# Expert outputs stored over the gathered rows, sixteen row buffers, and the late row scatters in one block

## The reference, cut to what matters

```python
probs = softmax(xt @ gate_w + gate_b)
_, idx = top_k(probs, 2)                       # 2 of 8 experts for each token
mask = (one_hot(idx).sum(axis=1) > 0)
h1 = relu(einsum('th,ehf->etf', xt, w1) + b1[:, None, :])      # 128 -> 512
out_e = einsum('etf,efh->eth', h1, w2) + b2[:, None, :]        # 512 -> 128
out = einsum('eth,te->th', out_e, mask)
```

## Time and profile before

| what | value |
|---|---|
| times of three executions | 623.2, 623.84, 632.16 us |
| median | 623.84 us |
| the profiled execution's own time | 632.16 us (the only one that is not below its span) |
| its span, first to last instruction | 630.1 us |
| busy, share of the span | PE 80%, DVE 65%, ACT 46%, POOL 43% |
| experts, first layer | about 203 to 293.5 us of the span |
| experts, second layer | about 528 to 617.3 us |

### The profile page before, as it was taken

One profiled execution on the slowest core, in us unless ns is written; L12 is line 12 of the kernel. 1 busy time (PEld: TensorE's weight loads), 2 busy tenths in 40 slices (PEclk: granted clock), 3 DMA queues, 4 the chain that ended last, 5 costly groups with the idle time before them and its releaser, 6 DMA issues.

```text
span 630.1 us, 14208 instructions
## 1 busy us (share of the span) xinstructions
PE 502.2 (80%) x4416; PEld 402.7 (64%) x4416; DVE 411.6 (65%) x1351; ACT 290.4 (46%) x824; POOL 269.1 (43%) x358
## 2 busy tenths in 40 slices
PE   4889998999973999893248899889789775998890
PEld 3656665656542999893136677667566465998890
DVE  5778888868867454536968646957956776643333
ACT  2234455435541665664354456625625312656650
POOL 3325543356475445646001133322822654355550
PEclk9979999858985899997576879979878755999995
DMA  7997000000001212213997000000000002212216
GB/s 231 336 286 322 3 2 1 1 10 27 5 32 48 79 52 78 76 52 116 373 292 293 2 2 1 2 1 2 28 9 3 27 28 64 67 57 78 78 39 208
DMA packets 28376, 53.71 MB, mean 85 GB/s; under 512 B 4817, under 2 KB 24209, under 8 KB 27249
## 3 DMA queue, kind: packets, MB, share of 16 engines
q1 hardware_dynamic: 23216, 42.17, 20.9%
q0 software_dynamic: 4544, 9.45, 4.2%
q10 hardware_dynamic: 544, 1.20, 0.6%
HBM read 42.32 MB, written 29.81 MB: 114 GB/s over the span
## 4 chain that ended last, share of the span: by engine, by line
PE 34%; DVE 30%; issue 16%; POOL 12%; DMA 4%; ACT 2%; SPq 1%; DVEq 1%; POOLq 0%; ACTq 0%
POOL ybuf L745 10%; DVE negm L870 5%; PE ps L2099 3%; PE ps L1999 3%; DVE X L1372 2%; PE ps L2059 2%; DMA w<-ybuf 2%; PE ps L2083 2%; PE ps L1845 1%; PE ps L1855 1%; POOL xbuf L695 1%; DVE rsc L944 1%; PE ps L1881 1%; PE ps L1915 1%; PE ps L2007 1%
## 5 line engine op out<-in xcount | busy, mean ns | idle before, releaser
L1579 ACT ACTIVATE probs<-ps,w1s 128x128 f32<-128x128 f32 x312 | 89.4, 376 | 58.4 <-PE ps L1999 47.7
L745 POOL DMA_INDIRECT ybuf<-yt,xg x78 | 77.5, 994 | 69.3 <-DVE yt L1126 58.2
L1999 PE MATMUL ps<-xgT,w1s 128*128 128x128 f32 x624 | 88.3, 287 | 8.9 <-DVE w1s L1062 7.3
L1999 PEld LDWEIGHTS ps<-xgT,w1s 128*128 128x128 f32 x624 | 80.2, 201 | 11.9 <-ACT xgT L1570 10.0
L2007 PE MATMUL ps<-w,probs 128*128 x624 | 82.2, 276 | 0.0
L780 POOL TENSOR_SCALAR_AFFINE_SELECT probs<-probs 128x512 f32<-128x512 f32 x64 | 39.4, 640 | 95.7 <-ACT probs L1680 95.6
L695 POOL DMA_INDIRECT xbuf<-rsc,sloti x64 | 62.5, 976 | 40.3 <-DVE sloti L999 15.2
L2007 PEld LDWEIGHTS ps<-w,probs 128*128 128x128 f32 x624 | 75.6, 192 | 0.0
L870 DVE TENSOR_REDUCE negm<-ps 128x2 f32<-128x512 f32 (+1 forms) x96 | 60.3, 685 | 22.3 <-PE ps L1832 17.1
L1493 ACT ACTIVATE probs<-ps 128x512 f32<-128x512 f32 x96 | 51.2, 600 | 35.5 <-PE ps L1855 35.1
L640 POOL TENSOR_SCALAR_AFFINE_SELECT probs<-probs 128x512 f32<-128x512 f32 x64 | 39.2, 637 | 60.6 <-ACT probs L1493 59.7
(11 more groups left out here) (280 smaller groups left out, 1115.1 us busy)
## 6 DMA issues: line engine op xcount, KB each, us to landing
xbuf<-in_c_pads SPq DMA_DIRECT2D x16, 1122.0 KB, 18.1
xg<-xbuf SPq DMA_DIRECT2D x78, 66.0 KB
w<-in_w SPq DMA_DIRECT2D x2, 2064.0 KB, 34.1
w<-in_w SPq DMA_DIRECT2D x2, 2048.0 KB, 35.7
w<-ybuf SPq DMA_DIRECT2D x8, 512.0 KB, 5.5
ybuf<-yt,xg POOLq DMA_INDIRECT x78
probs<-in_c_sel ACTq DMA_DIRECT2D x2, 512.0 KB, 5.2
bias<-in_b SPq DMA_DIRECT2D x2, 512.0 KB, 30.6
```

The lines of the kernel that those rows point to most:

```text
L745: pool.indirect_dma_start(out=ybuf[l][:, :], out_offset=bass.IndirectOffsetOnAxis(ap=xg[n % AHEAD][:, D:D + 1].bitcast(I32), axis=0), in_= ...
L1579: ins = act.activation(hidT[n % 3][:, c * P:(c + 1) * P], ps[:, q, c * P:(c + 1) * P], ACT.Gelu if l == 0 else ACT.Relu, bias=w[:, FF + c: ...
L1999: mm = pe.matmul(ps[:, n % 2, c * P:(c + 1) * P], w[:, c * P:(c + 1) * P], xgT[n % 2][:], start=True, stop=True)
```

## The change

The `yt` buffers are gone: the bias addition writes the result of tile n over the gathered rows in `xg[n % AHEAD]`, columns 0 to 127, and the scatter takes data and row numbers from the same buffer. `AHEAD` goes from 12 to 16. DVE no longer waits for a scatter; POOL does in its place, before it sends tile n, for that of tile n - 8, because eight scatter semaphores are left. At step 4 POOL sends the four late row scatters in one block, ahead of its wait for tile 4, and then y scatters alone, each as soon as its copy is done and POOL is free. Three semaphores are dropped: the pads of both layers share one, the table `pairs` is counted with the weights (thresholds 6 become 7), and an unused one goes.

```diff
-AHEAD = 12
+AHEAD = 16
...
-CAUGHT_UP = (12, 16, 20, 24)
...
-        yt = [sb(f"yt{r}", [P, D]) for r in range(DEPTH)]
...
-                sp.dma_start(xbuf[l][E * REGION:, :], inp["c_pads"][E * REGION:, :]).then_inc(pads_out[l], 16)
+                sp.dma_start(xbuf[l][E * REGION:, :], inp["c_pads"][E * REGION:, :]).then_inc(pads_out, 16)
...
-                pool.wait_ge(w_loaded[0], 16 * 6)
+                pool.wait_ge(w_loaded[0], 16 * 7)
...
                 def scatter_y(n):
+                    pool.wait_ge(m["y_copied"], n + 2)
                     pool.wait_ge(gathered[n % AHEAD], loads(l, n))
+                    if scatters(l, n % DEPTH, n // DEPTH) > 0:
+                        pool.wait_ge(scattered[n % DEPTH], scatters(l, n % DEPTH, n // DEPTH))
                     pool.indirect_dma_start(out=ybuf[l][:, :], out_offset=bass.IndirectOffsetOnAxis(ap=xg[n % AHEAD][:, D:D + 1].bitcast(I32), axis=0),
-                                            in_=yt[n % DEPTH][:], in_offset=None).then_inc(scattered[n % DEPTH], 16)
-
-                behind = 0
+                                            in_=xg[n % AHEAD][:, 0:D], in_offset=None).then_inc(scattered[n % DEPTH], 16)
+
                 for n in range(ET):
-                    pool.wait_ge(m["y_copied"], n + 2)
-                    if 0 <= n - LATE_ROWS < TOPK * size(LATE):
-                        t, k = divmod(n - LATE_ROWS, TOPK)
-                        ready_row(l, TILES[LATE][0] + t, LATE)
-                        scatter_row(l, TILES[LATE][0] + t, k)
-                        behind += 1
-                    else:
-                        scatter_y(n - behind)
-                    if n in CAUGHT_UP:
-                        behind -= 1
-                        scatter_y(n - behind)
+                    if n == LATE_ROWS:
+                        for t in range(*TILES[LATE]):
+                            scatter_rows(l, t, LATE)
+                    scatter_y(n)
...
                 def copy_y(n):
                     e = of_tile.pop(n)
                     dve.wait_ge(m["y_ready"], n + 2)
-                    if scatters(l, n % DEPTH, n // DEPTH) > 0:
-                        dve.wait_ge(scattered[n % DEPTH], scatters(l, n % DEPTH, n // DEPTH))
-                    dve.tensor_tensor(yt[n % DEPTH][:], ps[:, 6 + n % 2, 0:D], bias[:, ds(e * D, D)], ALU.add).then_inc(m["y_copied"], 1)
+                    dve.tensor_tensor(xg[n % AHEAD][:, 0:D], ps[:, 6 + n % 2, 0:D], bias[:, ds(e * D, D)], ALU.add).then_inc(m["y_copied"], 1)
```

More of the change, by code:

```diff
@@ L310, in build @@
         rows_out = [sem(f"rows_out{q}") for q in range(4)]
-        pads_out = [sem(f"pads_out_{l}") for l in range(2)]
-        pairs_loaded = sem("pairs_loaded")
+        pads_out = sem("pads_out")
         gathered = [sem(f"gathered{r}") for r in range(AHEAD)]
@@ L338, in build @@
         stats_done = sem("stats_done")
-        rstd_step = sem("rstd_step")
         stored = sem("stored")
@@ L556, in fill @@
                     rows_e = slice(e * REGION, (e + 1) * REGION)
-                    sp.dma_start(xbuf[l][rows_e, :], inp["c_pads"][rows_e, :]).then_inc(pads_out[l], 16)
-                sp.dma_start(xbuf[l][E * REGION:, :], inp["c_pads"][E * REGION:, :]).then_inc(pads_out[l], 16)
-            sp.dma_start(pairs[:].rearrange("p t k -> p (t k)"), inp["c_pairs"][:, :]).then_inc(pairs_loaded, 16)
+                    sp.dma_start(xbuf[l][rows_e, :], inp["c_pads"][rows_e, :]).then_inc(pads_out, 16)
+                sp.dma_start(xbuf[l][E * REGION:, :], inp["c_pads"][E * REGION:, :]).then_inc(pads_out, 16)
+            sp.dma_start(pairs[:].rearrange("p t k -> p (t k)"), inp["c_pairs"][:, :]).then_inc(w_loaded[0], 16)
             fill(0)
@@ L717, in _ @@
                 if (c, s) == (2, 2):
-                    pool.wait_ge(pairs_loaded, 16)
                     rank_constants()
@@ L723, in _ @@
                     if t == 0:
-                        pool.wait_ge(pads_out[0], 16 * (E + 1))
+                        pool.wait_ge(pads_out, 16 * (E + 1))
                     scatter_rows(0, t, q)
@@ L792, in _ @@
                         if t == 0:
-                            pool.wait_ge(pads_out[1], 16 * (E + 1))
+                            pool.wait_ge(pads_out, 2 * 16 * (E + 1))
                         scatter_rows(1, t, q)
@@ L1772, in gate_rows @@
                 if q == 0:
-                    pe.wait_ge(w_loaded[l], 16 * (6 if l == 0 else 4))
+                    pe.wait_ge(w_loaded[l], 16 * (7 if l == 0 else 4))
                 pe.wait_ge(m["rT_copied"], sum(rT_banks(a) for a in range(q + 1)) + 1)
```

## The result

The changed kernel takes 627.57 us (median of 20 runs, 622.67 to 634.57) against 624.25 us for the kernel before in the same measurement (20 runs, 617.29 to 632.16). The ratio is 1.0056, 95% interval [1.003, 1.0082]: a little slower, by less than 1%, 3.3 us between the medians, where 3.3 us faster was forecast. 627.57 lies above the range of 616 to 626. Medians in this document are of all executions, while a ratio leaves out those that lie more than 1.5% above the fastest of their kernel, so the two can disagree.

What follows compares the result with a forecast made beforehand. PE was taken to bound the expert stages at 1.90 us a tile. Gaps gained 7.3, less 3.8 for the long bunch and 0.2 for waits, gave 3.3 us: 623.84 - 3.3 = 620.5 us, range 616 to 626.

Steps and rivals of the forecast that it cites:

- Which engine bounds the stage: Expert stages: PE is always busy, one tile each 1.90 us; POOL keeps up and waits for DVE's copies.
- sizes of the bunch: POOL, once a layer: four late rows and y scatters, ten in a row at 1.26 us, 12.6 us.
- The term of 7.3 us for the eight gaps: PE's four gaps a layer at the catch-up steps vanish with the bunches of three scatters: 7.3 us gained at most.
- rival (1): Expert stages: gaps not from bunches in ordinary executions, nothing on the path changes, 623 to 624.5 us; 0.27 with (4).
- (4): Expert stages: the block goes before y4, nothing else moves; same time as rival (1), 0.27 together.
- The term of 3.8 us for the long bunch: Ten-scatter bunch beside PE: priced as two small gaps of 0.9 us, 1.9 us a layer, 3.8 us lost.
- rival (2): Long bunch holds PE's signals to its end: 5.0 us idle a layer, +2.9 us, 626.7; chance 0.13.
- Gaps of the triples did not add up within one: Argument against rival (2), from the gaps beside bunches of three scatters at the catch-up steps; no size.
- Most of it falls in the stretch that DVE's routing paces: Long bunch: mostly where DVE's routing sets 2.03 rather than 1.90 us a tile, so no more than 1.9 a layer.
- The terms at nothing: Gather lead, earlier late rows, merged semaphores and storing over gathered rows: 0 us each.
- The rule on the shared port: POOL's long bunch: each of six weight copies by DVE could add about half a microsecond, making no tile later.
- rival (3): Long bunch costs nothing and small gaps go too: 7.3 + 1.5 - 0.2 = 8.6 us gained, 615.2 to 617; chance 0.15.

Runs made afterwards that it cites:

- block only: Kernel before with POOL's new order alone (late row scatters in one block, then each y scatter as soon as copied), chip 7: 632.18 us, ratio 1.0069.
- old places: Changed kernel with four row buffers and a spacer placed so every other buffer lies where it lay before, chip 7: 638.35 us, ratio 1.0173.
- single rows: Changed kernel with late row scatters sent one by one at steps 4, 6, 8 and 9: 626.31 us on chip 15, 635.67 on chip 13.

## Why the prediction was wrong

**Which engine bounds the stage, and the sizes of the bunch: right.** POOL waits for DVE's copies as before (31.8 us in 31 waits against 29.5 in 24), the late rows and y scatters go at 1.26 us, and POOL has caught up about where 226.7 + 1.26 j = 222.0 + 2.03 j puts it: in the first profile after, four rows and seven y scatters run in a row from 234.41 before POOL waits 0.43 us, against ten scatters foreseen. No trace has a wait of DVE for a scatter, no turn of a tile in the later part of a stage waits for its gather, and the waits for gathers at the start add up to 0.7 us for 0.5.

**The term of 7.3 us for the eight gaps: the step that failed.** "3.6 + 3.7 = 7.3 us at most, if all of these gaps come from them" was taken at full size, and "I carry the difference over" made it the gain of every run. The gaps are real (on chips 7 and 13, too, a layer of POOL's old order has four, or two or three and one without a releaser), and where the triples go they go. But on chips 15, 9 and 5 no trace of either kernel has one, with the kernel before shown there on chip 9. There nothing can be won, and the kernel before shown with 83.5 and 82.3 us had no gap to lose. The one profile at hand came from a chip of the kind with gaps, or from an execution like it; the sign was in the text, the 8.3 us that the profiled execution stood above the median, and I gave the case built on it, rival (1), 0.27 together with (4). By the pair of chips 13 and 9 the kernel before differs by 633.97 - 624.59 = 9.4 us, and its expert stages by (87.8 + 87.1) - (83.5 + 82.3) = 9.1: most of the difference lies in these two stages (the stages are of single executions, which differ by 635.04 - 624.29 = 10.75 us), 6.2 us of it in gaps by a staged copy.

**The term of 3.8 us for the long bunch: too small where it counts.** Taken as two small gaps, 1.9 us a layer. On the chips that hold signals it measured 3.5 and 4.0 us (block only), 3.4 and 4.5 (old places), 4.3 and 4.6 (changed, chip 13). Rival (2) had this right, and nearly in detail: a bunch of six scatters, 6 x 1.26 = 7.6 us, for which 549.03 to 556.35 measured 7.3, and 5.0 us of idle PE, for which 4.3 and 4.6 stand. "Gaps of the triples did not add up within one" was no argument against it. "Most of it falls in the stretch that DVE's routing paces" failed too: in the second layer on chip 13 DVE stood idle for 4.90 us while PE's signals stood out, so its routing did not hide the gap.

What rival (2) lacked was the clock: the group behind the gap takes 2.05 us for 1.06. PE's busy time by stage shows what that costs. On chip 13, both layers, first the kernel before, then the changed one (columns as above):

```profile
209.00:297.00 88.00, 81.22 (x702) 78.71 (x702) 42.36 (x136) 56.36 (x201) 46.67 (x48) 0.96 0.22 65
531.00:618.00 87.00, 80.53 (x702) 78.39 (x702) 36.02 (x124) 51.63 (x196) 45.09 (x48) 0.97 0.23 65
...
212.00:300.00 88.00, 80.23 (x702) 77.89 (x702) 42.77 (x138) 56.58 (x201) 46.25 (x49) 0.97 0.24 66
531.00:621.00 90.00, 82.39 (x702) 81.06 (x702) 36.41 (x126) 51.94 (x196) 44.58 (x48) 0.93 0.23 63
```

In the second layer the gaps by a staged copy grew by 1.9 us, one of 0.93 us went, and the same 702 matmuls took 82.39 - 80.53 = 1.9 us more at the lower clock: 2.9, and the stage grew by 89.7 - 87.1 = 2.6. In the first layer the long gap came in two parts, 2.87 and 1.42 us, the clock stayed at 1.00 from 232 to 252, and PE's work was 1.0 us shorter, since the stage began at a granted clock of 0.88 (212 to 232) where the kernel before had 0.83 (209 to 229). The gaps grew by 0.8 and the stage shrank by 0.3. So in this pair of executions the long bunch cost 0.8 and 1.0 us more of idle PE than the small gaps had, and the larger loss is the clock of the second layer.

**The sum, as it came out.** On chips that hold signals: the small gaps gone, the large ones in their place, and on chip 13 the changed kernel is 3.6 us slower by medians against the 29 runs beside it and 4.5 against the 12 of the kernel before profiled with it; rival (2) worked out +2.9. On chips that hold none the medians lie 0.8 (chip 15), 0.5 (chip 9; 1.6 against the kernel before profiled there) and 0.9 (chip 5) apart, rival (1)'s zero to within what the runs can tell, with the same sign each time. The first measurement, +3.3, lies between the two kinds. The sign of the forecast would have needed a long bunch that costs less than the gaps it removes, on a chip that has gaps at all; no chip showed that.

**The terms at nothing: right, as far as they can be read.** Semaphores alone leave gaps and stages as they were (87.5 and 87.1 us); storing over the gathered rows alone too (87.7 and 86.5); old places do not bring the gaps back or drive them out. The extra wait on POOL, put at 0.1 us a layer, cannot be seen in any of these times.

**The rule on the shared port: there, but small.** The forecast let weight copies stretch the bunch by up to half a microsecond each. In the changed kernel's first profile, first layer, three scatters of the bunch took 1.17, 1.10 and 1.05 us and all others 0.95 to 0.98, 0.44 us more in all. What parts them is which of the two started first (timelines of DVE and POOL):

```profile
236.99 0.43 DVE L1052 COPY w1s<-w 128x516 f32 x1 [0.47 <-issue]
237.14 1.10 POOL L691 DMA_INDIRECT xbuf<-rsc,sloti  x1 [0.30 <-issue]
...
238.54 0.95 POOL L691 DMA_INDIRECT xbuf<-rsc,sloti  x1 [0.30 <-issue]
238.94 0.43 DVE L1052 COPY w1s<-w 128x516 f32 x1 [0.47 <-issue]
```

The scatter of 237.14 began inside a copy that ended at 237.42 and took 0.14 us more than 0.96. The scatter of 238.54 was under way when its copy began, and lost nothing. The other two long ones, at 234.41 and 247.40, began inside copies as well, and so did the one of 253.97 inside the addition of the earlier trace rows; all four end 0.82 to 0.83 us after the DVE operation does. The Trainium skill, SBUF - State Buffer, section "SBUF: two separate sides", lets GpSimd's descriptors wait until DVE's copy has ended. The trace agrees for a scatter that begins inside a copy; the price is what is left of the copy, 0.22 to 0.34 us here less some 0.13, and not half a microsecond for each copy beside the bunch.

**The chances and one term.** They do not add up as written: the halves of (2) and (3) that were left out come to 0.14 and not to two tenths, and for the 1.5 us in the sum of rival (3) the row behind it gives 1.1. Neither changes which case came out.

**What stays open.** Why some chips hold PE's signals beside a run of indirect scatters and others do not: it goes with the chip in every measurement here (held on 7, 3 and 13, free on 15, 9 and 5), but each chip was seen once. That the scatters hold them is argued from the order: on chip 7 POOL's order alone turned four small gaps in a layer into one long one at the new bunch. A kernel without bunches was never run on a chip of the first kind; both tries fell on chips 15 and 5. That single rows make the longest gap shorter (2.1 us and, in the second layer, 1.7, against 2.9 and 4.6 on chip 13; 635.67 us against 638.51) agrees with it. Which chips the first twenty runs of each kernel came from is not known, nor whether the 0.5 to 0.9 us on the free chips are anything (on chip 9 the interval of the ratio leaves 1 out, on chips 15 and 5 it does not). No version that I tried beats the kernel before: single rows are at 626.31 against 625.95 on chip 15 and at 635.67 against 634.92 on chip 13.

## What to carry to other kernels

A gap in one profile is a gain only if ordinary executions have it: where the profiled execution stands above the median by about as much as the gaps that you mean to remove, profile the same kernel again, on another chip too, before you build on them. Two profiles from different chips must not be subtracted stage by stage; a stage that the change can't touch (here the first attention, +13.3 us) is the control, and when it moves, the pair is no comparison. And where back-to-back indirect DMAs coincide with late signals, keep them apart: on the chips with late signals, four small bunches made into one long one gave a gap of up to 4.6 us, behind which TensorE ran at half its clock, and sending the rows one by one took back 2.8 of the 4.5 us lost on chip 13 (638.51 to 635.67 us, 633.97 before).

## What the runs showed of the hardware that I had not expected

- On some chips signals from TensorE reach ScalarE and VectorE late beside runs of GpSimd's indirect scatters: 0.7 to 1.1 us of idle PE for three in a row, 2.0 to 4.6 us in one gap for six and more, ACT starting up to 6.1 us after the modelled end of its matmuls, in one case 5.3 us after it and 0.1 us before the last scatter's end. On others, with the same program and scatters 1.26 us apart, no such gap stands and ACT is never over 0.73 us late.
- The same program takes 624 to 626 us on one kind of chip and 633 to 635 on the other, before any change.
- A gap of 4.6 us in TensorE's work was followed by a granted clock of 0.50: 2.05 us for eight matmuls that take 1.06 us at full clock.
- A scatter that begins inside a weight copy of VectorE is stretched by what is left of the copy less some 0.13 us (1.17, 1.10 and 1.05 us for 0.96); one that is under way when the copy begins is not (0.95).
- The first attention took 203.2 us at a granted clock of 0.87 and 216.5 at 0.80, untouched by the change, and 216.4 at 0.81 in a kernel that has none of it. Run by itself it took 218.61 us in one kernel and 218.85 in the other.
